# Flamingo block with sparsemax attention: the last excess measurement of two tiles moved from ScalarE to GpSimd and VectorE

## The reference

```python
x = x + tanh(g_xattn) * xattn(layernorm(x), ctx, ctx)   # 16 heads, keys 1601
x = x + tanh(g_ffn) * moe(layernorm(x))                 # 8 experts, top 2

def sparsemax(x):
    x = x - max(x)
    zs = sort(x, descending)
    cssv = cumsum(zs) - 1.0
    k = count(zs > cssv / rho)
    tau = cssv[k - 1] / k
    return clip(x - tau, 0.0)
```

## Time and profile before

| what | us |
|---|---|
| median of 3 executions | 7428.7 (7425.35 to 7432.42) |
| profiled execution, its own time | 7425.23 |
| span of that execution, first to last instruction | 7423.3 |
| busy: TensorE matmul | 5646.4 (76%) |
| busy: VectorE | 5977.4 (81%) |
| busy: ScalarE | 5842.5 (79%) |
| busy: GpSimd | 2210.4 (30%) |

### The profile page before, as it was taken

How to read it: one execution, slowest core, us unless ns; L and a number is a source line. 1 busy time by engine, 2 the same in 40 slices (tenths; PEclk the granted TensorE clock), 3 DMA queues, 4 the chain that set the end, 5 groups by cost and what they waited for, 6 DMA issues and landing times. The chain is left out here.

```text
span 7423.3 us, 165050 instructions
## 1 busy us (share of the span) xinstructions
PE 5646.4 (76%) x20864; PEld 1924.1 (26%) x20864; DVE 5977.4 (81%) x49467; ACT 5842.5 (79%) x13220; POOL 2210.4 (30%) x10037
## 2 busy tenths in 40 slices
PE   8976777776777777767777777677777775999999
PEld 5541111111111111111111111111111111666666
DVE  5559989999998999999999999899999995444443
ACT  2328999999999999999999999899999996222222
POOL 2223333333333333333333333333333332000000
PEclk9986666666666666666666666666666666999999
DMA  6651111111111111111111111111111112111110
GB/s 203 225 194 30 30 30 31 32 30 30 33 31 31 30 31 30 30 29 30 30 32 30 32 30 33 27 31 32 31 32 31 33 33 62 49 37 48 51 37 23
DMA packets 315591, 344.02 MB, mean 46 GB/s; under 512 B 113912, under 2 KB 238464, under 8 KB 314240
## 3 DMA queue, kind: packets, MB, share of 16 engines
q1 hardware_dynamic: 311936, 324.40, 15.9%
q0 software_dynamic: 2304, 8.39, 0.3%
HBM read 212.38 MB, written 120.10 MB: 45 GB/s over the span
## 5 line engine op out<-in xcount | busy, mean ns | idle before, releaser
L856 DVE MAX8 a_cand<-a_scores 128x8 f32<-128x42 f32 (+1 forms) x38912 | 4359.1, 193 | 296.2 <-issue 222.9
L619 ACT ACTIVATE a_junk_act<-a_cand,a_ntau 128x304 f32<-128x304 f32 (+1 forms) x4096 | 2066.8, 522 | 112.3 <-POOL a_ntau L931 50.5
L589 PE MATMUL a_ring<-a_q,a_k 99*128 99x512 bf16 (+1 forms) x3328 | 1478.7, 560 | 800.7 <-ACT a_scores L654 594.2
L534 PE MATMUL a_out<-a_attn,a_v 128*16 128x512 f32 (+1 forms) x6656 | 1404.2, 767 | 575.2 <-ACT a_attn L658 575.2
L654 ACT COPY a_scores<-a_ring 128x1024 f32<-128x1024 f32 (+1 forms) x2048 | 1612.2, 830 | 176.8 <-PE a_ring L585 110.1
L658 ACT ACTIVATE a_attn<-a_ring 128x1024 f32<-128x1024 f32 (+1 forms) x1792 | 1653.4, 974 | 2.5 <-PE a_ring L589 2.0
L585 PE MATMUL a_ring<-a_k,a_q 96*128 96x512 bf16 (+1 forms) x4096 | 1393.6, 471 | 71.6 <-DVE a_ident L679 32.9
L619 ACT ACTIVATION_READ_ACCUMULATOR a_junk_act<-a_cand,a_ntau 128x1 f32 x4096 | 845.6, 206 | 0.0
L585 PEld LDWEIGHTS a_ring<-a_k,a_q 96*128 96x128 bf16 x4096 | 391.9, 118 | 1472.7 <-issue 696.5
L589 PEld LDWEIGHTS a_ring<-a_q,a_k 99*128 99x128 bf16 (+1 forms) x3328 | 290.1, 119 | 1669.7 <-ACT a_scores L654 978.9
L1192 ACT ACTIVATE e_hid<-e_hid_ps,e_b_in 128x512 f32<-128x512 f32 x256 | 173.1, 687 | 667.7 <-PE e_hid_ps L1139 667.4
(11 more groups left out here) (171 smaller groups left out, 5777.0 us busy)
## 6 DMA issues: line engine op xcount, KB each, us to landing
a_k<-k_parts SPq DMA_DIRECT2D x1536, 50.0 KB
k_parts<-p_ks SPq DMA_DIRECT2D x48, 800.5 KB, 7.5
o_parts<-a_o SPq DMA_DIRECT2D x1024, 32.0 KB, 1.6
e_o<-o_parts SPq DMA_DIRECT2D x64, 512.0 KB, 6.6
p_ctx<-in_ctx_t SPq DMA_DIRECT2D x16, 1601.0 KB, 8.5
v_heads<-p_v SPq DMA_DIRECT2D x16, 1536.0 KB
a_q<-q_parts SPq DMA_DIRECT2D x1536, 16.0 KB
a_v<-v_heads SPq DMA_DIRECT2D x256, 96.0 KB
```

The lines of the kernel that those rows point to most:

```text
L534: mm = nc.tensor.matmul(out_ps[at:at + HEAD_DIM], v_st[0:rows, u, c], attn[0:rows, k, (c % 2) * BANK:(c % 2 + 1) * BANK], start=c < 4, sto ...
L589: mm = nc.tensor.matmul(at[0:rows, m * BANK:(m + 1) * BANK], k_st[0:SCORE_ROWS + TAU_ROWS, ut, c * P:c * P + rows], q_st[0:SCORE_ROWS + TA ...
L619: ins = nc.scalar.activation(into[:, t].rearrange("p (a b) -> p a b", b=CHUNKS), cand[:, u % SLOTS, t, 0:w], ACT.Relu, bias=ntau[:, u % 2, ...
L856: ins = V.max(cand[:, u % SLOTS, t, :, c], scores[:, u % SLOTS, t, lo:hi])
```

## The change

ScalarE's round 3 now covers tiles 0 and 1 only (`ACT_LAST = 2`). For tiles 2 and 3 GpSimd makes max(cand - tau, 0) as a full array of 304 numbers (`above`) in `last_excess`, and adds it up by folding: 304 to 152, to 76, to 38, to 19 numbers per tile. VectorE adds the last 19 in one TENSOR_REDUCE, which stands in tile 1 of its step, behind five links and thus behind six pairs of MAX8. `last_step` waits for it. In tile 2, `settle` stands five links later than before.

```diff
+ACT_LAST = 2
...
-                for t in range(TILES):
+                for t in range(ACT_LAST if r == ROUNDS - 1 else TILES):
...
                 def beside(t):
 
                     last, prev = (u - 2) % U, (u - 1) % U
+                    if t == 1 and has(i, 2):
+
+                        for _ in range(5):
+                            yield
+                        dve.wait_ge(part_summed, i - 1)
+                        V.tensor_reduce(excess[:, last % 2, ROUNDS - 1, ACT_LAST:], above_part[:], AX.X, ALU.add).then_inc(last_summed, 1)
+                        yield
...
                     if t == 2 and has(i, 2):
+                        for _ in range(5):
+                            yield
                         yield from settle(i - 2, last, link)
...
+                def last_excess(i, u):
+
+                    pool.wait_ge(tau_tried, (ROUNDS - 1) * (i + 1))
+                    pool.sem_inc(passed_pool, 1)
+                    for t in range(ACT_LAST, TILES):
+                        ins = G.tensor_scalar(above[:, t - ACT_LAST], cand[:, u % SLOTS, t].rearrange("p a b -> p (a b)"), ntau[:, u % 2, t:t + 1], 0.0, ALU.add, ALU.max)
+                    link(ins)
+                    for w in (CAND // 2, CAND // 4, CAND // 8):
+                        link(G.tensor_tensor(above[:, :, 0:w], above[:, :, 0:w], above[:, :, w:2 * w], ALU.add))
+                    w = CAND // 16
+                    G.tensor_tensor(above_part[:], above[:, :, 0:w], above[:, :, w:2 * w], ALU.add).then_inc(part_summed, 1)
+
                 def last_step(i, u):
 
                     nt = ntau[:, u % 2]
+                    pool.wait_ge(last_summed, i + 1)
+                    pool.sem_inc(passed_pool, 1)
                     pool.wait_ge(excess_made, ROUNDS * i + ROUNDS)
...
                 if has(i, 2):
+                    last_excess(i - 2, (u - 2) % U)
                     last_step(i - 2, (u - 2) % U)
```

More of the change, by code:

```diff
@@ L433, in attend_program @@
         own_excess = sb("own_excess", [P, TILES])
+        above = sb("above", [P, TILES - ACT_LAST, CAND])
+        above_part = sb("above_part", [P, TILES - ACT_LAST, CAND // 16])
         count4 = sb("count4", [P, TILES])
@@ L470, in attend_program @@
         excess_made = sem("excess_made")
+        part_summed = sem("part_summed")
+        last_summed = sem("last_summed")
         fall_made = sem("fall_made")
@@ L869, in _ @@
             G = nc.gpsimd
-            FIRST_LINKS, LAST_LINKS = 6 + 4 + 5, 5 + 3
+            FIRST_LINKS, LAST_LINKS = 6 + 4 + 5, 4 + 5 + 3
             def links_before(i):
```

## The result

The changed kernel takes 8390.63 us (median of 4, 8387.54 to 8392.59) where the kernel before takes 7429.03. The ratio is 1.129, with a 95% interval of 1.1275 to 1.1314: 962 us, 13%, slower. The profiled execution has a span of 8385.6 us.

A forecast was written before the change was run, and what follows sets the result against it. Before, ScalarE and VectorE are nearly full; after, a ring through ScalarE, VectorE and GpSimd sets the pace: 24.33 + 0.5 = 24.8 us, 255 steps, 6324 us, plus 90 for passes; attention +773, so 8200 us, range 8010 to 8400.

The forecast's parts named there:

- the ring: Closed chain through ScalarE's rounds, VectorE's sum, GpSimd's `last_step` and `second`, back to round 1: 24.33 us a step against 22.12.
- the hold: VectorE's four L699 in `start` meet GpSimd's folds and wait for the rest of one: 0.5 us a step.
- steps 5 to 7: VectorE's reduction and handover to GpSimd 0.36 us; `last_step` and first instruction of `second` 2.62; rest of `second` to round 1 2.91.
- step 3: VectorE after the fall: rest of tile 3 and one pair of tile 0, up to `start`'s opening, 3.12 us.
- 24.3 to 25 us between openings of `start`: Sign expected in the new profile: the length of a step, measured between openings of `start`.
- step 4: VectorE from the opening of `start` through tile 0 to the place of the sum in tile 1: 8.27 us.
- Cover of `last_excess`: GpSimd's `last_excess` ends by 13.8 us after round 1's start, VectorE asks at 18.5: 4.7 us to spare.
- Unsettled tiles: Extra passes in the attention stage: 1.5 us for one in a step, 7.0 for two, 90 us taken in all.
- No hold (8080): Rival: VectorE isn't held by GpSimd; 24.33 us a step, +653 us, 8080 us; chance 0.33.
- every fold a hold (8550): Rival: VectorE is held by all of GpSimd's folds; 26.17 us a step, +1122 us, 8550 us; chance 0.09.
- VectorE never falls behind ScalarE (7800): Rival: GpSimd's fall comes in time for VectorE; 23 us a step, +374 us, 7800 us; chance 0.04.
- VectorE would be the bound: Rival: the new sum is ready before needed; 20.3 + 0.1 us a step, 247 us of passes, 7235 us; chance 0.03.

The follow-up runs named there:

- the wait alone: Changed kernel with ScalarE measuring all tiles, `last_excess` gone, VectorE's sum reading a constant, `last_step` still waiting for it: 8234.47 us, ratio 1.109.
- second first: Changed kernel with GpSimd's `second` of item i-1 put ahead of `last_step` of item i-2: 7720.95 us, ratio 1.040.
- count later: Changed kernel with `second` ahead of `last_step`, and TensorE's count of `bad` moved behind the pieces of group 3: 7439.09 us, ratio 1.0019.

## Why the prediction was right, and where its sizes were off

The forecast was 8200 us in a range of 8010 to 8400, slower, by the ring with VectorE held by GpSimd for 0.5 us. The result, 8391, lies at the upper end. The direction and the mechanism were right and are shown: the wait alone makes 811 us, and taking it off the ring (second first, count later) gives back 951. These are the sum's terms, in us a step; median and mean are over 253 steps of the changed kernel. The recorded terms add up to 24.35, not 24.33, and with the hold to 24.85, which was rounded to 24.8; over 255 steps that is 13 us too few.

| term | predicted | median | mean |
|---|---|---|---|
| 1 round 1 to the end of round 2 | 6.28 | 6.28 | 6.32 |
| 2 to VectorE's fall | 0.79 | 0.79 | 1.07 |
| 3 to the opening of `start` | 3.12 | 3.12 | 3.44 |
| 4 to the sum, with the hold | 8.27 + 0.5 | 8.58 | 8.68 |
| 5 to `last_step` | 0.36 | 0.53 | 0.53 |
| 6 to `second` | 2.62 | 2.77 | 2.77 |
| 7 to round 1 | 2.91 | 2.92 | 3.10 |
| whole step | 24.85 | 25.27 | 25.90 |

- **The terms that were mis-sized are steps 5 to 7 of the sum and, most of all, step 3, for which I took a quiet step for all steps.** Steps 5 and 6 came out 0.17 and 0.15 us longer. At both places GpSimd has two waits to pass, where I had taken the handover from waits for a single semaphore; that this is the reason is my reading, and no run varied it. Step 3 is 5.1 us instead of 3.1 once in six steps, 40 times in all, where VectorE's program, written out for six items, jumps back to the start of its loop: I had read a step in the middle of the loop. That is 0.32 us in the mean, 82 us in all. Step 7 is 3.10 in the mean, but in half of the excess it is the unsettled tiles again: in 16 steps with a pass it is 1.7 us longer, and without passes its mean is 3.00. In the steps without a pass a step takes 25.56 us in the mean, 0.71 more than 24.85: step 3 gives 0.34, steps 5 and 6 0.32 and step 7 0.09, the rest are smaller, and the hold takes 0.09 back. 0.71 us are 180 of the 190 us by which the forecast was short. My sign "24.3 to 25 us between openings of `start`" was missed too: it is 25.27 in the median and 25.87 in the mean.
- **The hold of VectorE by GpSimd**, the term without a row before, is there, and somewhat smaller than the 0.5 us that I took: the stretch of step 4 takes 8.22 us in the median of the run with the wait alone, where GpSimd folds nothing, and 8.58 in the changed kernel (8.24 and 8.68 in the mean). It sits in three places of `start`. The four measures at L704 start within 0.71 instead of 0.64 us, the four at L709 within 1.00 instead of 0.88, and the 4-column L732, 143 ns in before, takes 312 (min/median/max ns, the changed kernel and then before):

```profile
L732 DVE SCALAR_TENSOR_TENSOR a_w<-a_w x256: 134/312/687, 567.5 to 7165.4; 128x4 f32<-128x4 f32 x128
```

```profile
L727 DVE SCALAR_TENSOR_TENSOR a_w<-a_w x256: 132/143/183, 569.0 to 6209.9; 128x4 f32<-128x4 f32 x128
```

  0.07 + 0.12 + 0.17 = 0.36 us. By the rule of the Trainium skill ("SBUF — State Buffer", SBUF: two separate sides) VectorE's instructions with two SBUF inputs are locked out for a GpSimd instruction that reads SBUF and started first. For the folds, which have two inputs, the trace of the change agrees: in 220 of 256 steps L732 met the first fold (0.83 us long), which had started before it, and ended 0.02 us behind the fold's end. For the one-input L905 it doesn't: as far as the profile's spans of GpSimd, which are rough, can tell, 965 of the 1024 instructions of L704 began and ended while one L905 of 1.33 us was running, with a median of 288 ns. Only the first of each four was longer, 342 ns where it was 280 before. All of L704:

```profile
L704 DVE SCALAR_TENSOR_TENSOR a_junk<-a_cand,a_ntau,a_zeros x1024: 272/288/586, 565.8 to 7164.6; 128x76 f32<-128x76 f32 x171
```

  So my picture of one long hold, the rest of one fold, was not what came: it is several short ones, and that they add up to about my 0.5 us is in part luck.
- **Cover of `last_excess`.** I gave its one-input instructions 0.24 to 0.77 us; they take 1.33. My upper end, the two-input price, was no bound: on GpSimd this one-input instruction is dearer than a two-input add of the same width (0.83 us). It did no harm to the forecast only because the cover was so large: 4.7 us of it became 3.48 in the step shown.
- **Unsettled tiles.** One pass in a step was to cost 1.5 us, two 7.0. Measured, against the mean of the quiet steps of the same kernel: 1.3 and 7.5, 88 us in all where I took 90.
- **The waits named beforehand** are all there, with no wait of VectorE for the partial sums but the very first, 7.5 us: ScalarE before round 1 (4 us forecast, 3.9 in the step shown, 4.7 in the mean), VectorE's two (2 and 2 forecast, 2.20 and 2.16 in the step shown).
- **The rivals.** No hold (8080) and every fold a hold (8550) are out by step 4. That VectorE never falls behind ScalarE (7800) is out by its waits for the fall, 232 of them in the waits view above. That VectorE would be the bound and the time fall to 7235 is out by the ring; and its price was wrong as well. I took VectorE's own time from a quiet step, 20.4 us, and left out the loop's end and the hold; the run with the count later, where VectorE is nearly the bound, gives 21.84 with the unsettled passes, where the rival's 20.4 and its 247 us of passes make 21.4.

Open: GpSimd stops for about 3 us ahead of the first instruction of `last_excess` 40 times (L905, put down to "issue", 118.5 us in all). It does so always in the first of the six steps of a pass through its loop, so the stop goes with the loop's end; what the engine does in it no run shows.

## What to carry to other kernels

In a hand-written pipeline an engine with 70% idle time can still be on the path, if every instruction of it stands in one fixed order: before adding a wait to such an engine, list what is queued behind the waiting instruction and when the consumer of each wants it; here the consumer had 0.14 us to spare. When an operation is split over two engines, look for a place to hand it back at which nothing urgent is queued behind the receiver's wait, and test the order before the work: moving one instruction by five pairs gave 234 us, turning two functions round gave 670. And take the length of a ring from all steps, the loop's end among them, not from a quiet one.

## What the runs showed of the hardware that I had not expected

- A GpSimd TENSOR_SCALAR of 304 float32 columns takes 1333 ns with a per-row operand and two operations, 1249 with constants, 1066 with one operation, where the TENSOR_TENSOR add that writes as many columns takes 826.
- VectorE's SCALAR_TENSOR_TENSOR on just 4 columns goes from 143 to 312 ns, since it is held to the end of the 304-column fold that it meets. The one of 152 columns goes from 369 to 416 ns where a fold of 152 columns started first, and to 931 where it was the one of 304. Beside the one-input TENSOR_SCALAR of 1333 ns the one of 76 columns keeps its 288 ns in the median.
- Stops for unsettled tiles that are half hidden in a kernel with a slow ring come back into the time when the ring is shortened: 14 pairs of 0.21 us gave 634 us, not 750. The stops at the loop's end don't: those steps are 1.7 us longer than the others in both kernels.
